# Two mixture-of-experts stages of a long kernel, their 64 experts taken one by one and in pairs

## The reference, cut to what matters

```python
buf = jnp.zeros((NUM_EXPERTS, CAPACITY, H), x.dtype).at[se, rank].set(x[st], mode='drop')   # 64, 160, 128
h = jnp.einsum('ech,efh->ecf', buf, expert_w1)                                              # 768 wide
x1, x2 = jnp.split(h, 2, axis=-1)
out = jnp.einsum('ecf,ehf->ech', x1 * jax.nn.silu(x2), expert_w2)
y = out[se, jnp.clip(rank, 0, CAPACITY - 1)]
y = jnp.where(valid[:, None], y * sw[:, None].astype(y.dtype), 0.0)
combined = jnp.zeros((T, H), x.dtype).at[st].add(y)
```

## Time and profile before

| | |
|---|---|
| median of three runs | 3925.31 us |
| profiled execution | 3935.15 us |
| its span | 3933.4 us |
| busy in the span | PE 2708.0, PEld 1753.0, DVE 2212.2, POOL 1920.1, ACT 1409.4 us |
| granted clock of TensorE, mean | 0.824 |
| scatters of `experts` in `l0f1`, `l0f2` | 128 each, 179.7 and 178.8 us of POOL |
| hidden products of one of these stages | 768 instructions, 118.5 us of PE |

### The profile page before, as it was taken

The page is one execution under the profiler, slowest core; times in us unless marked ns, Lnnn a source line. Parts: engine busy times, 40 slices in busy tenths (PEclk is TensorE's granted clock), DMA queues, the critical chain, the costliest instruction groups (busy, mean ns, idle before and its releaser), DMA issues. The chain is left out here.

```text
span 3933.4 us, 70148 instructions
## 1 busy us (share of the span) xinstructions
PE 2708.0 (69%) x24900; PEld 1753.0 (45%) x24900; DVE 2212.2 (56%) x5951; ACT 1409.4 (36%) x2942; POOL 1920.1 (49%) x2400
## 2 busy tenths in 40 slices
PE   3339937633797454799967999471688875999471
PEld 2228824422686142555544555361233332555361
DVE  6752347567333444367743675414599997675413
ACT  1112204211121313346532565132667661566131
POOL 4767740077386212257742111566588784111565
PEclk7769968677899687889987899585799997899586
DMA  9108941110488442000000100132112110010132
GB/s 338 47 6 203 226 111 35 46 65 17 107 230 198 175 135 115 9 16 17 15 7 12 20 17 11 53 88 57 76 54 86 52 78 12 18 19 11 52 86 77
DMA packets 231098, 294.78 MB, mean 75 GB/s; under 512 B 36614, under 2 KB 187527, under 8 KB 224656
## 3 DMA queue, kind: packets, MB, share of 16 engines
q1 hardware_dynamic: 176912, 246.21, 20.4%
q0 software_dynamic: 47616, 39.44, 5.0%
q10 hardware_dynamic: 6272, 5.24, 0.5%
HBM read 182.43 MB, written 107.12 MB: 74 GB/s over the span
## 5 line engine op out<-in xcount | busy, mean ns | idle before, releaser
L3378 PE MATMUL l3am_y<-l3am_hc,ident 128*128 128x512 f32 x512 | 280.4, 631 | 95.6 <-DVE l3am_hc L3287 95.5
L3067 POOL TENSOR_TENSOR l3am_db<-l3am_du,l3am_bs 128x512 f32<-128x512 f32 x256 | 317.9, 1272 | 43.6 <-DVE l3am_hh L3279 43.6
L3279 DVE TENSOR_TENSOR_SCAN l3am_hh<-l3am_dA,l3am_db 128x512 f32<-128x512 f32 x256 | 301.4, 1214 | 48.2 <-ACT l3am_dA L3187 47.0
L777 POOL TENSOR_TENSOR l2a_pT<-l2a_pT,kept 128x512 int32<-128x512 int32 x192 | 241.6, 1272 | 116.5 <-ACT l2a_pT L992 115.8
L879 DVE CUSTOM_DVE_ANT_0 l2a_junk<-l2a_s,addend 128x256 f32<-128x256 f32 x512 | 187.4, 421 | 82.0 <-PE l2a_s L1106 68.5
L2460 POOL DMA_INDIRECT l0f_table<-l0f2e_y,l0f2e_idx x128 | 178.8, 1397 | 103.7 <-DVE l0f2e_idx L2432 57.6
L2054 POOL DMA_INDIRECT l0f_rows<-l0f1r_row,l0f1r_idx x160 | 172.7, 1079 | 94.0 <-issue 94.0
L2460 POOL DMA_INDIRECT l0f_table<-l0f1e_y,l0f1e_idx x128 | 179.7, 1404 | 67.0 <-issue 32.2
L872 DVE TENSOR_REDUCE l3f2a_mx<-l3f2a_s 128x2 f32<-128x512 f32 x256 | 165.6, 686 | 67.5 <-PE l3f2a_s L1106 66.2
L872 DVE TENSOR_REDUCE l3f1a_mx<-l3f1a_s 128x2 f32<-128x512 f32 x256 | 165.6, 686 | 67.2 <-PE l3f1a_s L1106 66.0
L3378 PEld LDWEIGHTS l3am_y<-l3am_hc,ident 128*128 128x128 f32 x512 | 91.2, 194 | 227.8 <-DVE l3am_hc L3287 176.7
(11 more groups left out here) (749 smaller groups left out, 7120.4 us busy)
## 6 DMA issues: line engine op xcount, KB each, us to landing
l3am_bs<-l3a_b SPq DMA_DIRECT2D x32, 1024.0 KB, 4.7
l0f1m_w<-in_L_ffn_expert_w SPq DMA_DIRECT2D x64, 384.0 KB, 3.2
l0f2m_w<-in_L_ffn_expert_w SPq DMA_DIRECT2D x64, 384.0 KB, 3.2
l0f_rows<-blank SPq DMA_DIRECT2D x8, 1930.0 KB, 21.6
l0f1m_w<-in_L_ffn_expert_w SPq DMA_DIRECT2D x64, 192.0 KB, 3.6
l0f2m_w<-in_L_ffn_expert_w SPq DMA_DIRECT2D x64, 192.0 KB, 3.6
l1a_top<-l1a_kernel SPq DMA_DIRECT2D x12, 1024.0 KB, 11.9
l3f_rows<-blank SPq DMA_DIRECT2D x8, 1440.0 KB, 11.1
```

Source lines behind the costliest of these rows:

```text
L777: self.nc.gpsimd.tensor_tensor(t, t, self.kept[:, f // 8 % 2, :].unsqueeze(1).to_broadcast([P, 2, 2 * P]), ALU.mult).then_inc(self.cut_g, 1)
L3067: G.tensor_tensor(db[j][n % 2][:, :], du[j][k % 2][:, :], bs[s // QUARTER][:, s % QUARTER, :], ALU.mult).then_inc(db_ready[j], 1)
L3279: V.tensor_tensor_scan(hh[j][n % 2][:, :], dA[j][n % 2][:, :], db[j][n % 2][:, :], 0.0, ALU.mult, ALU.add).then_inc(h_ready, 1)
L3378: T.matmul(yb[j][:, :], c.ident[:, :], hc[j][n % 2][:, :], start=(s == 0), stop=(s == N - 1)).then_inc(summed, 1)
```

## The change

The 64-expert stages get a function of their own, `paired_experts`, and `experts` keeps only the 8-expert stages, whose instructions stay the same. The step is now a pair of experts, 32 pairs unrolled by four. The 320 rows of a pair are three pieces: the first 128 rows of one expert, the first 128 of the other, and a third of 64 that holds the last 32 of both. Both tables are one HBM tensor; expert one of a pair adds to the first table and expert two to the second, by an offset that is added to the index on VectorE, so that the mixed piece goes to both. The scatters are sent in the order piece 0, mixed piece, piece 1. Piece 0 waits for pieces 0 and mixed of the pair before, the mixed piece for piece 1 of the pair before. Eight experts' weights are held in place of four; the four weight loads of a pair stand ahead of its three row loads in SyncE's queue. The output products of the mixed piece use 32 columns at column positions 0 and 32. VectorE computes the gated values of pair n+1 at the beginning of step n, ahead of index and y of pair n.

```diff
-        if self.apart:
-            self.all_tables = nc.dram_tensor(f"{name}_tables", (TABLES * TABLE, D), F32, kind="Internal").ap()
-            self.tables = [self.all_tables[i * TABLE:(i + 1) * TABLE, :] for i in range(TABLES)]
-        else:
-            self.tables = [nc.dram_tensor(f"{name}_table{i}", (TABLE, D), F32, kind="Internal").ap()
-                           for i in range(TABLES)]
+        self.all_tables = nc.dram_tensor(f"{name}_tables", (TABLES * TABLE, D), F32, kind="Internal").ap()
+        self.tables = [self.all_tables[i * TABLE:(i + 1) * TABLE, :] for i in range(TABLES)]
...
+def paired_experts(nc, c, name, m, mats, E, CAP, C1, KC):
+    rows = m.rows
+    with Phase(nc, name) as ph:
+        R, S, F = m.R, CAP, KC * CAP
+        U, RING, REST = 4, 4, CAP - P
+        PIECES = (P, P, 2 * REST)
+        pairs = E // 2
+        assert REST == 32 and mats.places == 2 * U
+        row = [ph.sb(f"row{i}", [P, 3, R]) for i in range(U)]
+        xeT = [ph.sb(f"xeT{i}", [P, 2 * S]) for i in range(2)]
+        sT = [ph.sb(f"sT{i}", [P, F]) for i in range(2)]
+        gT = [[ph.sb(f"gT{i}{q}", [P, F]) for q in range(2)] for i in range(2)]
+        y = [ph.sb(f"y{i}", [P, 3, D]) for i in range(RING)]
+        idx = [ph.sb(f"idx{i}", [P, 3], U32) for i in range(RING)]
+        table = ph.sb("table", [P, 3])
...
+        @block.sync
+        def _(sp):
+            def load(i, u):
+                n = U * i + u
+                if not isinstance(n, int) or n >= U:
+                    sp.wait_ge(y_ready, n - U + 1)
+                    for q in range(2):
+                        mats.load(sp, 2 * n + q, 2 * u + q)
+                both = rows[bass.ds(2 * S * n, 2 * S), :].rearrange("(q s) r -> s q r", q=2)
+                sp.dma_start(row[u][:, 0:2, :], both[0:P, :, :]).then_inc(loaded[u], 16)
+                for q in range(2):
+                    sp.dma_start(row[u][REST * q:REST * (q + 1), 2, :], both[P:S, q, :]).then_inc(loaded[u], 16)
+            for u in range(U):
+                load(0, u)
+            with sp.Fori(1, pairs // U) as i:
+                for u in range(U):
+                    load(i, u)
+        @block.tensor
+        def _(pe):
+            def turn(i, u, n):
+                pe.wait_ge(loaded[u], 48 * (i + 1))
+                if not first(n):
+                    pe.wait_ge(xe_ready, n)
+                for a, k in enumerate(PIECES):
+                    mm = nc.tensor.transpose(xb[:, a * P:a * P + k], row[u][0:k, a, 0:D], c.ident[0:k, 0:k])
+                mm.then_inc(turned, 1)
+            def hidden(i, u, n):
+                pe.wait_ge(xe_ready, n + 1)
+                for q in range(2):
+                    e = 2 * u + q
+                    pe.wait_ge(mats.loaded[e], mats.LOADED * (i + 1))
+                    if not first(n):
+                        pe.wait_ge(g_ready, 2 * n + q - 1)
+                    for f in range(C1):
+                        mm = nc.tensor.matmul(hb[q][f // 3][:, (f % 3) * S:(f % 3 + 1) * S],
+                                              mats.t1[e][:, f * P:(f + 1) * P], xeT[u % 2][:, q * S:(q + 1) * S],
+                                              start=True, stop=True)
+                    mm.then_inc(h_done, 1)
+            def output(i, u, n):
+                p = u % 2
+                pe.wait_ge(g_ready, 2 * n + 2)
+                if not isinstance(n, int) or n >= 2:
+                    pe.wait_ge(y_ready, n - 1)
+                def part(f, q, start, length, piece, place):
+                    return nc.tensor.matmul(ob[p][place:place + length, piece * D:(piece + 1) * D],
+                                            gT[p][q][:, f * S + start:f * S + start + length], mats.t2[2 * u + q][:, f, :],
+                                            start=(f == 0), stop=(f == KC - 1), tile_position=(0, place),
+                                            skip_group_check=True)
+                for q in range(2):
+                    for f in range(KC):
+                        part(f, q, 0, P, q, 0)
+                for f in range(KC):
+                    for q in range(2):
+                        mm = part(f, q, P, REST, 2, REST * q)
+                mm.then_inc(o_done, 1)
+            def step(at):
+                if at(1):
+                    hidden(*at(1))
+                if at(2):
+                    turn(*at(2))
+                output(*at(0))
+            turn(0, 0, 0)
+            hidden(0, 0, 0)
+            turn(0, 1, 1)
+            stream(pe, pairs, U, step)
+        @block.scalar
+        def _(a_):
+            def copy(i, u, n):
+                a_.wait_ge(turned, n + 1)
+                x3 = xeT[u % 2][:, :].rearrange("p (q s) -> p q s", q=2)
+                nc.scalar.activation(x3[:, :, 0:P], xb[:, 0:2 * P].rearrange("p (q s) -> p q s", q=2), ACT.Copy)
+                nc.scalar.activation(x3[:, :, P:S], xb[:, 2 * P:2 * S].rearrange("p (q s) -> p q s", q=2), ACT.Copy
+                                     ).then_inc(xe_ready, 1)
+            def step(at):
+                i, u, n = at(0)
+                for q in range(2):
+                    a_.wait_ge(h_done, 2 * n + q + 1)
+                    if not first(n):
+                        a_.wait_ge(g_ready, 2 * n + q - 1)
+                    nc.scalar.activation(sT[q][:, :], hb[q][1][:, 0:F], ACT.Silu).then_inc(s_ready, 1)
+                if at(2):
+                    copy(*at(2))
+            copy(0, 0, 0)
+            copy(0, 1, 1)
+            stream(a_, pairs, U, step)
+        @block.vector
+        def _(v):
+            nc.vector.memset(table[:, :], 0.0).then_inc(table_made, 1)
+            v.wait_ge(table_made, 1)
+            nc.vector.memset(table[:, 1:2], float(TABLE)).then_inc(table_made, 1)
+            nc.vector.memset(table[REST:2 * REST, 2:3], float(TABLE)).then_inc(table_made, 1)
+            v.wait_ge(table_made, 3)
+            def gate(i, u, n):
+                for q in range(2):
+                    v.wait_ge(s_ready, 2 * n + q + 1)
+                    nc.vector.tensor_tensor(gT[u % 2][q][:, :], hb[q][0][:, 0:F], sT[q][:, :], ALU.mult).then_inc(g_ready, 1)
 
             def step(at):
                 i, u, n = at(0)
                 p = u % 2
+                if at(1):
+                    gate(*at(1))
+                if not isinstance(n, int) or n >= RING:
+                    for t in added:
+                        v.wait_ge(t, 16 * (n - RING + 1))
+                v.wait_ge(loaded[u], 48 * (i + 1))
+                r, d = row[u], idx[u]
+                nc.vector.tensor_tensor(d[:, 0:2], r[:, 0:2, R - 1], table[:, 0:2], ALU.add)
+                nc.vector.tensor_tensor(d[0:64, 2:3], r[0:64, 2, R - 1:R], table[0:64, 2:3], ALU.add).then_inc(idx_ready, 1)
+                v.wait_ge(o_done, n + 1)
+                for a, b, piece, q in ((0, P, 0, 0), (0, P, 1, 1), (0, REST, 2, 0), (REST, 2 * REST, 2, 1)):
+                    mm = nc.vector.tensor_scalar(y[u][a:b, piece, :], ob[p][a:b, piece * D:(piece + 1) * D],
+                                                 r[a:b, piece, bass.ds(D + 2 * n + q, 1)], None, ALU.mult)
+                mm.then_inc(y_ready, 1)
+            gate(0, 0, 0)
+            stream(v, pairs, U, step)
+        @block.gpsimd
+        def _(g):
+            last_row = g.to_reg(TABLES * TABLE - 1)
+            g.wait_ge(m.tables_cleared, m.TABLES_CLEARED)
+            def add(u, a):
+                k = PIECES[a]
+                g.indirect_dma_start(out=m.all_tables, out_offset=bass.IndirectOffsetOnAxis(ap=idx[u][0:k, a:a + 1], axis=0),
+                                     in_=y[u][0:k, a, :], in_offset=None, bounds_check=last_row, oob_is_err=True,
+                                     compute_op=ALU.add).then_inc(added[a], 16)
+            def step(at):
+                i, u, n = at(0)
                 hold(g, c.mark_g, idx_ready, n + 1)
                 hold(g, c.mark_g, y_ready, n + 1)
+                if not first(n):
+                    g.wait_ge(added[0], 16 * n)
+                    hold(g, c.mark_g, added[2], 16 * n)
+                add(u, 0)
+                if not first(n):
+                    hold(g, c.mark_g, added[1], 16 * n)
+                add(u, 2)
+                add(u, 1)
+            stream(g, pairs, U, step)
             for t in added:
+                g.wait_ge(t, 16 * pairs)
...
-        mats = Matrices(outer, w["L0_ffn_expert_w1"], w["L0_ffn_expert_w2"], 6, 3, 4)
+        mats = Matrices(outer, w["L0_ffn_expert_w1"], w["L0_ffn_expert_w2"], 6, 3, 8)
         route(nc, c, name + "r", w, c.x, m, "L0_ffn_wg", 64, 8, 160, "softmax", mats, shared=True)
-        experts(nc, c, name + "e", w, m, mats, 64, 6, 3, 2, True)
+        paired_experts(nc, c, name + "e", m, mats, 64, 160, 6, 3)
```

## The result

The changed kernel takes 3976.16 us (median of 4 runs, 3966.47 to 3997.13) against 3930.03 of the kernel before beside it (4 runs, 3924.92 to 3944.54): 1.0128 times as long, 95% interval 1.0094 to 1.0162. Forecast was 3886, with 3850 to 3930 as the range; the time lies above both, and above every rival's, the 3962 of (c) included.

The account below looks back on a forecast made before the run. In the expert stages GpSimd's scatters, row loads and TensorE ran at nearly one pace, 7.11 us a pair, to become 6.3. Gains of 22.3 and 19.7 less 3 for loads ahead gave -39, hence 3886 us; range 3850 to 3930.

Parts of the forecast that it names:

- (c): Rival: 128-row adding scatters cost by the row, 2.24 us each; pace 7.6 us a pair, 3962 us, chance 0.12.
- Issue of the scatters: GpSimd in the stages: three scatters a pair at 1.70 us each with gap, 5.11 us in place of 6.82.
- TensorE: Matrix work of a pair in the stages: 5.4 to 6.2 us, taken as 5.9, column tiles saving 0 to 0.8.
- Start of a stage: First pair does two experts' products before anything else: first y 7.0 us later, at 309.0.
- Loads ahead: Four more experts' weights loaded early in each routing: 0 to 10 us in stage one, taken as 3; nothing in stage two.
- VectorE: Under 3 us of a 6.3 us pair, y 1.1; hidden unless GpSimd falls four pairs (25 us) behind.
- Row loads: Rows last of seven loads after y: loop of 5.3 us a pair; TensorE waits under 0.3 a pair.
- rival (b): Rows come late in the stages, 5.8 us in place of 3.5: pace 6.5 a pair, 3898 us, chance 0.08.
- The landing chain: Scatter issue to first scatter allowed after its landing, 3.45 to 5.12 us, plus one 1.70 interval: 5.15 to 6.8 a pair.
- rival (a): Landing chain takes over: scatters keep the crowded 5.12 us turnaround, pace 6.8 a pair, 3908 us, chance 0.22.
- Rival (d): Fewer scatters, but DMA engines were the limit all along: pace stays 7.1 us a pair, 3928 us, chance 0.08.

Follow-up runs that it names:

- e1: Changed kernel with only the first eight experts' weights ever loaded, row loads kept: 6.17 / 6.16 us a pair (stage one / two).
- e9: Changed kernel with a pair's rows loaded first and its two experts' weights later, not one burst: 7.24 / 7.24 us a pair, 1.0033 of the kernel before.
- e10: e9 plus y and index buffers for eight pairs in place of four: 7.30 / 7.24 us a pair, 1.0034 of the kernel before.
- e8: Kernel before with eight places for weights and rows, two experts' loads sent in one burst after every second y: 8.30 / 8.21 us per two experts.
- e2: Changed kernel with mixed pieces added into two tables of their own, left out of the result: 6.36 / 6.34 us a pair.
- e13: Changed kernel with four tables, all cleared and added up: 6.22 / 6.27 us a pair, 3912.81 us, 0.9959 of the kernel before.
- e4: Changed kernel with each pair in four pieces of 80 rows, no mixed piece or 128-row scatters: 8.13 / 8.11 us a pair.
- e3: Changed kernel with eight places in place of four for y, rows and their semaphores: 7.40 / 7.38 us a pair.
- e5: Kernel before, unchanged, run again on another chip as a check of the chip: 7.12 / 7.06 us per two experts.
- e7: Kernel before with eight places for weights and rows, loads still one expert at a time: 7.38 / 7.32 us per two experts, 0.9835 of the kernel before.
- e11: e1 with VectorE's gated values computed in the pair's own step, after y of the pair before: 9.61 / 9.61 us a pair.

## Why the prediction was wrong

- *Issue of the scatters*: right. 1.42 for 64 rows, 1.55 for 128, so 5.42 a pair with three gaps of 0.30 (5.11 forecast). Rival (c), by the row, falls: 128 rows would have been 2.24.
- *TensorE*: 5.9 forecast, 6.20 measured where nothing waits (products of 312.35 and 318.55), and 6.17 in e1: the upper end of my bounds. The output of a pair takes 2.31, where two units' took 2.62, so column tiles give 0.3, not 0.8. The Trainium skill, TensorEngine Tiling (Array Packing), Key Properties, says a change of the tiling mode drains TensorE. Whether that took the rest of the gain is not shown, as no run here prices the drain by itself.
- *Start of a stage*: +8.9 in stage one and +6.6 in stage two, for +7.0. *Loads ahead*: +2.7 for 3. *VectorE*: y of a pair 1.21 for 1.1, hidden; but it waits 78.7 us for scatters four pairs back, since GpSimd does fall that far behind, which the prediction had named as the one case. *Row loads*: TensorE waits 24.9 us for them, 20 times, 0.8 a pair where my bound was 0.3: rival (b) happens too, but e9 and e10, which put the rows first, stay at 7.24 and 7.30, so it costs nothing beside the chain.
- *The landing chain*: the step that failed, and with it the forecast. Its form was right, one turn plus one interval. Its size was taken as "the low to middle part", 3.45 to 5.12, with 6.09 as the worst; under loads it is 6.6 in the two pairs shown and 6.45 in the median. With 8.2 a pair in the sum of rival (a), for 25 pairs, and 5.8 for six: 309.0 + 4.2 + 25 x 8.2 + 6 x 5.8 + 3.45 = 556.5, plus 1.9 for the start and 2.7 ahead of the stage = 561.1, where the combine starts at 562.1. So this one term holds the miss.
- *Why it was mis-sized*: the bounds came from rows of a kernel that sends three loads after each y. The prediction counted seven loads after each y, but priced them only for the rows at their end, not for the scatters that land among them, and reasoned that they had "mostly gone" when piece 1 is issued, 4.2 us after its y. Neither held: piece 1 leaves 26 to 27 us after its own y, amid the loads of a later pair, at 408.02, and the last of the seven at 409.89 and later. Besides, 5.12 was only the time that three scatters take to issue. It says that most landings were not later than that. Where a first scatter of before did wait for a landing, nine times in stage one, the turn was 5.61 to 6.09. The DMA queues of 409.6 to 412.0 (packets, MB, share):
```profile
q1 hardware_dynamic: 399, 0.77, 87.8%
q0 software_dynamic: 124, 0.06, 19.0%
```
- *Which part was the cause*: two things together. Loads lengthen the turn (e1), and lying in one burst they lengthen it more, by e8, where the kernel before goes from 7.38 to 8.30 through the burst alone. The chain passes the longer turn on, by e2 and e13, where it is broken and the pace is 6.2 to 6.4 under the same bursts. The mixed piece and the 128-row scatters are not needed for the loss: e4 has neither and runs at 8.1. How much of the turn is the burst and how much the rate of the loads stays open (e9, e10). Excluded: a lock through the ring of four (e3), the DMA engines' rate (e2), the chip (e5).
- *Rival (a)* named the mechanism, at 3908 and with a chance of 0.22; it took before's ordinary 5.12 for the crowded turn. Rival (d), at 3928, leaves out its own 3 us for the loads ahead (its terms give 3931), which changes nothing. The trace agrees with the rule that rival (a) leaned on (the Trainium skill, DMA: Bandwidth & Descriptors, SWDGE vs HWDGE vs iDMA: an engine takes its queues in turn): packets of scatters and loads move side by side in the rows above, and the landing of piece 1 takes 5.6 in the median of the 25 pairs under loads, 3.2 to 3.8 behind them.
- Still open: why eight places without a burst cost 8 to 9 us a stage (e7), and why they shorten the attention layer.

## What to carry to other kernels

Where scatters into one table wait for each other, write the cycle down as (issue to landing) plus the interval of whatever else goes to that table, and ask what each edit does to the landing, not only to the count of scatters. Batching two steps' loads doubles the burst that a small transfer may have to land in; a bound read from the unbatched kernel is then no upper bound. If the chain binds, more tables can be cheaper than they look: here two more cost 16 us a combine against 44 to 47 us a stage. And where a change is small beside the whole, read the stages one by one: code that nobody touched moved here by more than the net gain of the best kernel's stages.

## What the runs showed of the hardware

- An adding scatter costs GpSimd 1.42 us for 64 rows, 1.40 for 80 and 1.55 for 128. Its landing, by contrast, moves with the traffic. For 128 rows it is about 3.3 us after the issue with no loads (turn 4.07), and 5.6 in the median beside bursts of 1.43 MB (turn 6.45). With rows first and the weights later (e9, turn 5.62) an estimate is 4.9: the turn less the 0.7 to 0.8 by which turn and landing differ in the other two.
- In e11 TensorE stands still for 2.1 to 2.4 us a pair, and its granted clock is 0.85 over the stage where e1 has 1.00. The pair became 3.4 us longer, more than the wait itself.
- An untouched attention layer took 9 to 18 us less in every run with eight weight places than in those with four. The cause is not known; such a difference is as large as that of many edits here.
